# Two key groups in the two row halves of the array: score matmuls in pairs, three stack buffers, one reduction over two banks

## The chip, the core and the metric

One core of a Trainium2 chip runs the whole program. The metric is the device time of one execution in microseconds, the median of a few runs. TensorE (PE) multiplies matrices and writes to PSUM, which has eight banks of 512 float32 numbers on each of 128 partitions; VectorE (DVE), ScalarE (ACT) and GpSimd (POOL) compute element by element; SyncE (SP) here issues most DMAs. The engines run their own instruction streams in order and meet at semaphores.

## What is computed

Eight images of 256x256 with 32 text tokens each go through a wavelet gate, a first attention with an expert layer, a second attention with an expert layer. Each step adds to the residual `h`, 2304 tokens of 256 numbers. The change touches the second attention only, a grouped one: 16 query heads of 16 dimensions share 4 key/value groups.

```python
def _L1_attn_ref(x, Wq, bq, Wk, bk, Wv, bv, Wo, bo):
    ...
    q = (x @ Wq.T + bq).reshape(b, n, G, hpg, HD)
    k = (x @ Wk.T + bk).reshape(b, n, G, HD)
    v = (x @ Wv.T + bv).reshape(b, n, G, HD)
    scale = 1.0 / jnp.sqrt(jnp.float32(HD))
    scores = jnp.einsum('bqghd,bkgd->bghqk', q, k) * scale
    attn = jax.nn.softmax(scores, axis=-1)
    y = jnp.einsum('bghqk,bkgd->bqghd', attn, v).reshape(b, n, d)
    return y @ Wo.T + bo
```

Here b is 8 (images), n is 288 tokens, G is 4 groups, hpg is 4 heads a group, HD is 16.

## The kernel before

The second attention handles one image at a time, in a pipeline of turns (`turn(it)`), each of NU = 18 units U. In turn `it`, the projections of image `it` are made, the row maxima of image `it - 1`, the exponentials and value products of image `it - 2`, and the divisions of image `it - 3`. The same function `turn` stands in the stream of every engine, and the tables at the file's end (`PR_U`, `VT_U`, `MT_U`, `s_at`, `av_at`, ...) say in which unit each step stands. Turns 0 to 3 and 8 to 10 are written out, turns 4 to 7 are two passes of a loop of two turns.

The steps of an image:

- **Projection** (`project`, six matmuls each for m = 0, 1, 2, L1218 to L1220 by the helper `split3`) into bank 7, read by VectorE into `qf` (L1149); ScalarE rounds it to `qh` (L668) and GpSimd makes the rest `ql` (L462).
- **Stack.** SP writes `qh` and `ql` to DRAM (`scrH`, `scrL`, L337, L338) and reads them back as stacks `QS` (queries) and `KS` (keys), two buffers (L347, L350). A stack has three blocks of 16 rows (high x high, high x low, low x high), so one matmul over 48 rows is a product of near float32 precision; at `MROW` two more rows carry the row maxima and, in `KS`, minus ones. Before the change the matmuls use rows 0 to 95 or all 128, the unused rows being zeros that GpSimd wrote.
- **Row scores** (L1463): stationary 128 columns of `QS`, moving 288 keys, once for each of NS = 36 blocks of 128 query rows, alternately into banks 4 and 5. VectorE reduces each to a column of `MX` (L1139). Two transposes in units 5 and 14 (`MT_U`, L1510) bring the maxima to rows, VectorE splits them into `Mh` and `Ml` (L1154, L1156), and SP takes them through DRAM (`scrM`, L357) into the two rows at `MROW` of `QS` (L359).
- **Scores** (L1481): two a unit, stationary 96 keys, moving 384 queries, into banks 0 and 1 or 2 and 3 by turns. ScalarE reads both in one exponential (L661) into the ring `PR` of 12 slots.
- **Values** (L1524): for each of 12 steps m (group g, key tile kt) four matmuls of 32 columns, side by side in the column tiles, accumulate over kt in bank 6. After the third, ScalarE copies the group to `yr` (L715). The next group waits for that copy. A column of ones in `VA` gives the sums of the exponentials.
- **Division.** ScalarE's queue writes the sums to DRAM and reads them back (L692, L697), VectorE inverts (L1162), ScalarE's queue writes the inverses (L700) and reads them back spread over rows as `recb` in eight loads (L708), GpSimd multiplies and adds (L488, L491) into `yT`. The last image is divided on the way through a spreading matmul (L1505) and VectorE (L1169, L1172, L1177) instead. After six warming matmuls (L1226) the output projection (L1553) starts; it needs the `yT` of all images.

In the first turns (`early`) row scores use banks 4, 5, 0 and 1, and projections banks 2, 3 and 7. A unit's order on TensorE is: the score pair, one row score, values, projection, transposes, the other row score.

## Time and profile before

| | us |
|---|---|
| median of 3 runs | 867.09 |
| lowest and highest | 866.78 to 868.91 |
| the profiled execution | 867.73 |
| its span, first to last instruction | 866.0 |
| TensorE busy | 745.6 |
| VectorE busy | 599.9 |
| ScalarE busy | 347.5 |
| GpSimd busy | 146.6 |

The profile is one execution. A page gives busy times, digits of forty slices of the span and the costliest groups of instructions; the trace gives every instruction in order of time with what ended the idle time before it. Records of matmuls overlap, since they are pipelined, so the distance of two starts says more than a duration. PE is a matmul, PEld the load of its stationary operand. The second attention lies between 364 and 613 us.

### The profile page before, as it was taken

The page shows a single profiled execution, that of the slowest core. Times are in us where ns is not written, and L with a number is a line of the kernel's source. Part 1 is how long each engine was busy: PE and PEld are TensorE (multiplying, and loading weights), DVE is VectorE, ACT ScalarE, POOL GpSimd, SP SyncE. Part 2 cuts the span into 40 slices and gives each one's busy share as a digit, 9 for nine tenths or more (in the row PEclk, how much of TensorE's full clock was granted, in tenths as well). Part 3 has the DMA queues.
Part 4 walks back from the last instruction along what each step waited for, and adds up shares of the span by engine and source line. Part 5 has one row for each costly group of instructions (what it writes and reads, how often), then busy time and mean ns, then how long its engine had stood idle before and what let it go on. Part 6 is the DMA issues. An engine that isn't in the chain of part 4 may idle for free.

```text
span 866.0 us, 14451 instructions
## 1 busy us (share of the span) xinstructions
PE 745.6 (86%) x4818; PEld 631.8 (73%) x4818; DVE 599.9 (69%) x1377; ACT 347.5 (40%) x613; POOL 146.6 (17%) x136
## 2 busy tenths in 40 slices
PE   4549996899999996447999999998766899999997
PEld 4538994699999996335556655553544899999997
DVE  6396667677777778737777767763685777777776
ACT  1305543433333333102766666777155233333332
POOL 0105552000000001346013331112353000000000
PEclk9999996999999998556999999999878999999999
DMA  6300000000000000044345345321300000000000
GB/s 242 123 41 1 1 0 0 1 2 1 1 1 1 0 0 0 1 93 96 83 95 105 87 68 111 86 44 34 167 1 1 1 19 1 19 19 1 20 19 19
DMA packets 21559, 34.77 MB, mean 40 GB/s; under 512 B 6572, under 2 KB 17500, under 8 KB 20960
## 3 DMA queue, kind: packets, MB, share of 16 engines
q1 hardware_dynamic: 16632, 31.60, 13.9%
q10 hardware_dynamic: 4872, 2.46, 1.7%
q8 instruction: 32, 0.52, 0.3%
q14 instruction: 23, 0.19, 0.1%
HBM read 24.03 MB, written 9.99 MB: 39 GB/s over the span
## 4 chain that ended last, share of the span: by engine, by line
PE 72%; DVE 14%; DMA 4%; issue 3%; ACT 3%; POOL 2%; SPq 1%; ACTq 0%; POOLq 0%; DVEq 0%
PE PS L1218 16%; PE PS L1220 15%; PE PS L1219 15%; PE PS L1524 6%; PE PS L1463 5%; PE PS L1481 4%; DVE MX L1139 2%; PE PS L1247 2%; DMA KS<-scrH 1%; DMA scrL<-ql 1%; DVE nmr L1205 1%; PE PS L1306 1%; PE PS L1340 1%; PE PS L1226 1%; DVE stats L851 1%
## 5 line engine op out<-in xcount | busy, mean ns | idle before, releaser
L1139 DVE TENSOR_REDUCE MX<-PS 128x1 f32<-128x288 f32 x288 | 125.1, 452 | 51.7 <-PE PS L1463 48.5
L1071 DVE SCALAR_TENSOR_TENSOR h<-PS,cmb,h 128x256 f32<-128x256 f32 (+1 forms) x342 | 143.8, 476 | 0.3 <-PE PS L1220 0.3
L661 ACT ACTIVATE PR<-PS 96x768 f32<-96x768 f32 x144 | 115.4, 806 | 47.7 <-PE PS L1481 45.3
L629 ACT ACTIVATE sg<-PS 128x384 f32<-128x384 f32 x114 | 55.9, 491 | 166.4 <-PE PS L1220 166.4
L1463 PE MATMUL PS<-KS,QS 96*128 96x288 f32 x288 | 97.8, 360 | 17.9 <-DMA KS<-scrH 15.7
L1056 DVE TENSOR_TENSOR al<-aa,ah 128x384 fp32r<-128x384 f32 x114 | 63.7, 558 | 67.1 <-ACT ah L633 67.1
L1463 PEld LDWEIGHTS PS<-KS,QS 96*128 96x128 f32 x288 | 57.3, 203 | 60.1 <-DVE MX L1139 40.4
L633 ACT ACTIVATE ah<-aa 128x384 fp32r<-128x384 f32 x114 | 60.0, 526 | 83.6 <-DVE aa L1050 83.6
L1050 DVE TENSOR_TENSOR aa<-sg,PS 128x384 f32<-128x384 f32 x114 | 63.2, 555 | 26.5 <-ACT sg L629 25.9
L1220 PE MATMUL PS<-xTl,W1h 128*128 128x384 f32 x240 | 81.0, 337 | 0.0
L1218 PE MATMUL PS<-xTh,W1h 128*128 128x384 f32 x240 | 80.8, 337 | 0.0
L1219 PE MATMUL PS<-xTh,W1l 128*128 128x384 f32 x240 | 80.7, 336 | 0.0
L1481 PE MATMUL PS<-QS,KS 128*96 128x384 f32 x288 | 75.6, 347 | 1.9 <-DVE MX L1139 1.1
L1220 PE MATMUL PS<-xTl,W0h 128*128 (+1 forms) x216 | 73.6, 341 | 0.0
L1219 PE MATMUL PS<-xTh,W0l 128*128 (+1 forms) x216 | 73.3, 340 | 0.0
L1218 PE MATMUL PS<-xTh,W0h 128*128 (+1 forms) x216 | 73.3, 340 | 0.0
L1524 PE MATMUL PS<-PR,VA 128*32 128x288 f32 x768 | 66.3, 418 | 1.1 <-ACT yr L715 1.0
L1218 PE MATMUL PS<-W1h,ah 128*128 128x256 f32 x180 | 51.2, 284 | 4.0 <-DVE al L1056 4.0
L1220 PE MATMUL PS<-W1l,ah 128*128 128x256 f32 x180 | 51.0, 284 | 0.0
L1219 PE MATMUL PS<-W1h,al 128*128 128x256 f32 x180 | 50.6, 281 | 0.0
L1218 PE MATMUL PS<-W0h,ah 128*128 128x256 f32 x162 | 46.1, 285 | 4.4 <-DVE al L1056 4.4
L1481 PEld LDWEIGHTS PS<-QS,KS 128*96 128x96 f32 x288 | 42.2, 165 | 9.8 <-ACT PR L661 4.6
(233 smaller groups left out, 1567.4 us busy)
## 6 DMA issues: line engine op xcount, KB each, us to landing
QS<-scrH SPq DMA_DIRECT2D x32, 144.0 KB, 3.9
W1raw<-in_w SPq DMA_DIRECT2D x1, 3840.0 KB, 11.6
W0raw<-in_w SPq DMA_DIRECT2D x1, 3456.0 KB, 10.7
scrH<-qh SPq DMA_DIRECT2D x8, 432.0 KB, 2.5
scrL<-ql SPq DMA_DIRECT2D x8, 432.0 KB, 3.2
QS<-scrL SPq DMA_DIRECT2D x16, 144.0 KB, 4.5
out_tokens<-h SPq DMA_DIRECT2D x6, 384.0 KB, 2.4
x_in<-in_x SPq DMA_DIRECT2D x2, 1024.0 KB, 6.4
```

The costliest lines, as they stand in the source:

```text
L633: A_(ah[:, b], aa[:, b], ACT.Copy).then_inc(s[f"f{L}_ah"], 1)
L661: A_(PR[0:KT, c0:c0 + 2, :], PS[0:KT, b:b + 2, 0:CW], ACT.Exp).then_inc(s["e_exp"], 1)
L1050: V.tensor_tensor(aa[:, b], sg[:, b], PS[:, 2 + b, 0:GW], ALU.mult).then_inc(s[f"f{L}_mul"], 1)
L1056: V.tensor_tensor(al[:, b], aa[:, b], ah[:, b].bitcast(F32), ALU.subtract).then_inc(s[f"f{L}_al"], 1)
L1071: ins = V.scalar_tensor_tensor(out=hj, in0=PS[:, b + t // 2, (t % 2) * D:(t % 2) * D + D], scalar=cmb[:, ds(g * GT + t, 1), e:e + 1].squee ...
L1139: V.tensor_reduce(MX[:, c // NSH, c % NSH:c % NSH + 1], PS[:, max_bank(it, c), 0:POS], AX_X, ALU.max).then_inc(s["e_mx"], 1)
L1218: M(out_, wh, xh, start=(start and c == 0), stop=False)
L1219: M(out_, wl, xh, start=False, stop=False)
L1220: ins = M(out_, wh, xl, start=False, stop=(stop and c == n - 1))
L1463: M(PS[:, max_bank(it, c), 0:POS], QS[q][0:MROW, c * P:c * P + P], KS[q][0:MROW, c // 9 * POS:c // 9 * POS + POS], start=True, stop=True). ...
L1481: ins = M(PS[0:KT, n % 4, 0:CW], KS[p][:, g * POS + kt * KT:g * POS + kt * KT + KT], QS[p][:, g * HQ + cc * CW:g * HQ + cc * CW + CW], sta ...
L1524: ins = M(PS[32 * hh:32 * hh + 32, 6, 0:POS], VA[p][:, kt, g, :], PR[:, c0:c0 + 3, :].rearrange("p c w -> p (c w)")[:, hh * POS:hh * POS + ...
```

## The change

- **Row halves.** Stacks hold groups 0 and 1 in rows 0 to 49 and groups 2 and 3 in rows 64 to 113 (`TILE` = 64, `MROW` = 48), with half the columns. A score pair is now the same key tile and query columns of groups g and g + 2, each in its half of the array; a row-score pair is block c of both halves. The zeroing of the stacks on GpSimd is gone.
- **Maxima over two banks.** Row scores go in pairs to banks 4 and 5, one pair a unit, and one reduction over both banks writes two columns of `MX`, 9 apart. The next pair waits for it (`e_mx`). In the first turns pairs alternate between banks 4, 5 and 0, 1.
- **Three stack buffers** (`NQB`) and three `yr`. SP writes the minus ones of all three before the first stack, in both halves, reads both halves of a stack at a turn's end after all scores of the image that had the buffer, and reads the maxima back in two pieces.
- **Two rings** in `PR`, of 3 and 5 slots of three chunks; value products follow the order of groups `Y_G` = 0, 2, 1, 3 at the units `AV_U`.
- **Schedule.** Projections are made a turn earlier, in units 10, 12 and 14, so the stage has a turn -1; transposes of the maxima in units 6 and 16; the inverses are read back and the division done a turn later. All turns are written out.

```diff
-RING = 12
+NRA, NRB = 3, 5
+NQB = 3
 NS = NGQ * HQ // P
-MROW = 96
+TILE, MROW = 64, 48
...
-    QS = [seq(f"QS{p}", [P, NGQ * HQ], F32R, cur=k1) for p in range(2)]
-    KS = [seq(f"KS{p}", [P, NGQ * POS], F32R, cur=k1) for p in range(2)]
-    PR = seq("PR", [P, RING, CW], cur=k1)
+    QS = [seq(f"QS{p}", [P, NGQ // 2 * HQ], F32R, cur=k1) for p in range(NQB)]
+    KS = [seq(f"KS{p}", [P, NGQ // 2 * POS], F32R, cur=k1) for p in range(NQB)]
+    PR = seq("PR", [P, (NRA + NRB) * 3, CW], cur=k1)
...
+        for it in range(-1, IMGS + 1):
+            if live(it, 1):
+                max_rows(it - 1, 0)
+            if live(it, -1):
+                stack_out(it + 1)
+            if live(it, 1):
+                max_rows(it - 1, 1)
+            if live(it, -1):
+                if it < 0:
+                    sp.wait_ge(s["e_const"], 2)
+                    for p in range(NQB):
+                        minus_ones(p)
+                stack_in(it + 1, 0)
+                stack_in(it + 1, 1)
...
-                    old = (2 * U + 1 - RING) // 3
-                    wait(act, s["e_avt"], i * NAV + old + 1)
-                    c0 = (2 * U) % RING
+                    G = (i * NU + U) // 3
+                    if U % 3 == 0:
+                        ring_free(G, NRA, 0)
+                        ring_free(G, NRB, 1)
+                    ca, cb = ring_at(G, 0) + U % 3, ring_at(G, 1) + U % 3
                     b = 2 * (U % 2)
-                    A_(PR[0:KT, c0:c0 + 2, :], PS[0:KT, b:b + 2, 0:CW], ACT.Exp).then_inc(s["e_exp"], 1)
+                    A_(PR[0:KT, ca:cb + 1:cb - ca, :], PS[0:KT, b:b + 2, 0:CW], ACT.Exp).then_inc(s["e_exp"], 1)
...
+                if live(it, 4) and not last_image(it - 4) and U in RB_U and it < IMGS + 2:
+                    inverses_in(it - 4, RB_U.index(U))
+            if it == IMGS + 1:
+                for n in range(len(RB_U)):
+                    inverses_in(IMGS - 2, n)
...
+                k, c = s_at(U)
+                if live(it, k):
+                    i, hf = it - k, c // (NSH // 2)
+                    dve.wait_ge(s["e_s"], NSH * i + c + 1)
...
+                    b, z = max_bank(it, c), c % (NSH // 2)
+                    V.tensor_reduce(MX[:, hf, z:z + NSH // 2 + 1:NSH // 2], PS[:, b:b + 2, 0:POS], AX_X, ALU.max).then_inc(s["e_mx"], 1)
...
+        def scores(i, U):
+
+            g, kt, cc = U // 9, U % 9 // 3, U % 3
+            for a in range(2):
+                r = slice(TILE * a, TILE * a + MROW + 2)
+                ins = M(PS[0:KT, 2 * (U % 2) + a, 0:CW], KS[i % NQB][r, g * POS + kt * KT:g * POS + kt * KT + KT],
+                        QS[i % NQB][r, g * HQ + cc * CW:g * HQ + cc * CW + CW], start=True, stop=True, tile_position=(TILE * a, 0))
+            ins.then_inc(s["e_st"], 1)
+
+        def row_scores(i, c, bank):
+
+            g = c // (NSH // 2)
+            for a in range(2):
+                r = slice(TILE * a, TILE * a + MROW)
+                ins = M(PS[:, bank + a, 0:POS], QS[i % NQB][r, c * P:c * P + P], KS[i % NQB][r, g * POS:g * POS + POS],
+                        start=True, stop=True, tile_position=(TILE * a, 0))
+            ins.then_inc(s["e_s"], 1)
...
+                    wait(pe, s["e_mx"], NSH * i + c - (1 if early(it) else 0))
+                    row_scores(i, c, max_bank(it, c))
...
-PR_U = [0, 1, 2]
-VT_U = 3
-MT_U = [5, 14]
-
-SUM_U, SM_U, REC_U, RO_U, RB_U = [1, 2], 4, 7, 8, list(range(10, 18))
-S_LEAD = 8
+PR_U = [10, 12, 14]
+VT_U = 8
+MT_U = [6, 16]
+
+SUM_U, SM_U, REC_U, RO_U, RB_U = [6, 7], 11, 14, 16, list(range(4, 12))
+S_LEAD = 4
+
+Y_G = [0, 2, 1, 3]
+AV_U = [6, 7, 10, 11, 12, 13, 15, 17, 19, 20, 21, 22]
...
 def max_bank(it, c):
-    return (4, 5, 0, 1)[c % 4] if early(it) else 4 + c % 2
+    return (4, 0)[c % 2] if early(it) else 4
```

Three places of the order of instructions follow. In a row "L1441" is a line, then the operation, what it writes and reads, the size and how many stand in a row; a number behind QS or KS names the buffer. In the program after, L1432 are scores, L1441 row scores, L1456 values and L1195 to L1197 projections.

TensorE, before, a turn's first projections, with a score pair between two single row scores:

```order
L1481 MATMUL PS<-QS_140,KS_142 96x384 x2
L1463 MATMUL PS<-KS_141,QS_139 128x288
L1524 MATMUL PS<-PR,VA_144 32x288 x4
L1218 MATMUL PS<-xTh,a1h 128x288
L1219 MATMUL PS<-xTh,a1l 128x288
L1220 MATMUL PS<-xTl,a1h 128x288
...
L1463 MATMUL PS<-KS_141,QS_139 128x288
L1481 MATMUL PS<-QS_140,KS_142 96x384 x2
```

TensorE, after, units 10 and 11 of a turn and the start of unit 12:

```order
L1432 MATMUL PS<-QS_140,KS_143 96x384 x2
L1441 MATMUL PS<-KS_144,QS_141 128x288 x2
L1456 MATMUL PS<-PR,VA_147 32x288 x4
L1195 MATMUL PS<-xTh,a1h 128x288
L1196 MATMUL PS<-xTh,a1l 128x288
L1197 MATMUL PS<-xTl,a1h 128x288
...
L1432 MATMUL PS<-QS_140,KS_143 96x384 x2
L1441 MATMUL PS<-KS_144,QS_141 128x288 x2
L1456 MATMUL PS<-PR,VA_147 32x288 x4
L1432 MATMUL PS<-QS_140,KS_143 96x384 x2
```

The two single row scores of a unit have become a pair, and a value step, the first of a group, now stands one unit behind the projection.

SP, before, the start of the stage:

```order
L337 DMA scrH<-qh 128x864
L338 DMA scrL<-ql 128x864
L347 DMA QS_139<-scrH 16x8x288 x2
L347 DMA QS_139<-scrL 16x8x288
...
L350 DMA KS_141<-scrH 16x2x288
L332 DMA KS_141<-neg_158 2x1152
L332 DMA KS_142<-neg_158 2x1152
L337 DMA scrH<-qh 128x864
```

SP, after, the same place:

```order
L340 DMA scrH<-qh 128x864
L341 DMA scrL<-ql 128x864
L335 DMA KS_142<-neg_161 2x576 x2
L335 DMA KS_143<-neg_161 2x576 x2
L335 DMA KS_144<-neg_161 2x576 x2
L350 DMA QS_139<-scrH 16x8x288 x2
L350 DMA QS_139<-scrL 16x8x288
L354 DMA KS_142<-scrH 16x2x288
L354 DMA KS_142<-scrL 16x2x288
L354 DMA KS_142<-scrH 16x2x288
```

The minus ones, six loads instead of two, have moved from behind the first stack to ahead of it.

ACT, before, the end of the stage, the last inverses among the last exponentials:

```order
L715 ACTIVATE yr_155<-PS 128x288
L708 DMA recb<-scrR 16x2x288
L661 ACTIVATE PR<-PS 96x768
L708 DMA recb<-scrR 16x2x288
L661 ACTIVATE PR<-PS 96x768
L708 DMA recb<-scrR 16x2x288
L715 ACTIVATE yr_155<-PS 128x288
L739 ACTIVATE xnp<-h,nmr,rstd 128x256 x3
```

ACT, after, the same place (L646 is the exponential, L685 the write of the inverses, L699 their load, L705 the copy to `yr`):

```order
L646 ACTIVATE PR<-PS 96x2x384 x3
L685 DMA scrR<-rec 128x36
L646 ACTIVATE PR<-PS 96x2x384
L699 DMA recb<-scrR 16x2x288 x8
L705 ACTIVATE yr_157<-PS 128x288 x2
L724 ACTIVATE xnp<-h,nmr,rstd 128x256 x3
```

All eight loads of the inverses now stand between the last exponential and the last two copies.

## Rows read from the trace of the kernel before

**Rows 1.** The page: granted TensorE clock in forty slices, tenths of full.

```profile
PEclk9999996999999998556999999999878999999999
```

**Rows 2.** Grouped view: what, count, busy us, mean ns, idle before, releasers.

```profile
L661 ACT ACTIVATE PR<-PS 96x768 f32<-96x768 f32 x144 | 115.4, 806 | 47.7 <-PE PS L1481 45.3
...
L1524 PE MATMUL PS<-PR,VA 128*32 128x288 f32 x768 | 66.3, 418 | 1.1 <-ACT yr L715 1.0
```

**Rows 3.** Timeline of TensorE, one unit: start, length, engine, line, what, count.

```profile
446.10 0.69 PE L1524 MATMUL PS<-PR,VA 128*32 128x288 f32 x8
446.72 0.40 PE L1463 MATMUL PS<-KS,QS 96*128 96x288 f32 x1
446.96 0.51 PE L1481 MATMUL PS<-QS,KS 128*96 128x384 f32 x2
447.31 0.29 PE L1463 MATMUL PS<-KS,QS 96*128 96x288 f32 x1
447.54 0.69 PE L1524 MATMUL PS<-PR,VA 128*32 128x288 f32 x8
```

**Rows 4.** Timeline at the same place: reductions and next load, idle before.

```profile
447.16 0.94 DVE L1139 TENSOR_REDUCE MX<-PS 128x1 f32<-128x288 f32 x2 [0.49 <-PE PS L1463]
...
448.15 0.19 PEld L1463 LDWEIGHTS PS<-KS,QS 96*128 96x128 f32 x1 [0.47 <-DVE MX L1139]
```

**Rows 5.** Timelines of TensorE, VectorE and ACT: a projection and its followers.

```profile
434.61 0.40 PE L1218 MATMUL PS<-xTh,a1h 128*128 128x288 f32 x1
...
435.53 0.30 PE L1463 MATMUL PS<-KS,QS 96*128 96x288 f32 x1
...
435.73 0.52 DVE L1149 TENSOR_SCALAR qf<-PS,bq 128x288 f32<-128x288 f32 x1 [1.00 <-PE PS L1220]
...
436.29 0.44 ACT L668 ACTIVATE qh<-qf 128x288 fp32r<-128x288 f32 x1 [1.11 <-DVE qf L1149]
436.64 0.39 ACT L715 ACTIVATE yr<-PS 128x288 f32<-128x288 f32 x1
```

**Rows 6.** Chain that ended last, the stage's start: start, length, what.

```profile
371.15 3.17 DMA scrL<-ql
376.60 4.65 DMA KS<-scrH
381.30 3.22 PE PS L1463 x9
...
400.88 0.62 PE PS L1463
...
405.32 0.93 PE PS L1481 x2
```

**Rows 7.** Timeline of SP's queue at the stage's start.

```profile
377.07 0.90 SPq L347 DMA_DIRECT2D QS<-scrH  x2
...
379.89 1.36 SPq L332 DMA_DIRECT2D KS<-neg  x2
...
391.36 0.37 SPq L337 DMA_DIRECT2D scrH<-qh  x1
```

**Rows 8.** Timeline, the last turn's start and the stage's end.

```profile
583.71 0.95 PE L1481 MATMUL PS<-QS,KS 128*96 128x384 f32 x4
...
602.30 0.59 PE L1481 MATMUL PS<-QS,KS 128*96 128x384 f32 x2
602.73 0.65 PE L1505 MATMUL PS<-yr,spread 128*128 128x288 f32 x2
...
603.42 1.96 DVE L1169 RECIPROCAL qf<-PS 128x288 f32<-128x288 f32 x1 [2.16 <-PE PS L1505]
...
608.07 1.30 PE L1505 MATMUL PS<-yr,spread 128*128 128x288 f32 x2 [3.58 <-DVE qf L1172]
...
613.00 7.17 PE L1553 MATMUL PS<-wo,yT 128*128 128x256 f32 x30
```

**Rows 9.** DMA view: issues, KB each, median us from issue to landing.

```profile
scrR<-rec ACTq DMA_DIRECT2D x7, 18.0 KB, 1.9
```

More of the change, by code:

```diff
@@ L237, in build @@
     xn1 = at("xn1", [P, 2, GT, D], F32, k1[0])
-    yr = [seq(f"yr{p}", [P, NGQ, POS], cur=k1) for p in range(2)]
+    yr = [seq(f"yr{p}", [P, NGQ, POS], cur=k1) for p in range(3)]
     SW = NGQ * HPG * POS // P
@@ L725, in _ @@
+        for it in range(-1, IMGS + 3):
+            turn(it)
         n1 = sum(WCOLS[1]) // NG
@@ L1466, in turn @@
+        def turn(it):
+            for U in range(NU):
                 if live(it, 2):
@@ L1531, in _ @@
         pe.wait_ge(s["e_hi"], NG)
-        for it in range(4):
-            turn(it, it % 2)
-        with pe.Fori(2, 4) as r:
-            last[0] = ("e_msplit", 2 * (2 * r - 1))
-            turn(2 * r, 0)
-            turn(2 * r + 1, 1)
-        last[0] = ("e_msplit", 14)
-        for it in range(8, 11):
-            turn(it, it % 2)
+        for it in range(-1, IMGS + 3):
+            turn(it)
         warm_up(3)
```

344 lines of the change are left out of this document (146 added, 198 removed).

## Prediction

> **What bounds the kernel now.** I read the page first, then the timeline of the second attention, engine by engine. That stage runs from 364 to 613 us; nothing outside it is edited. Its clock is full except at its start: the digits of PEclk fall in slices 16 to 19 (of 21.65 us) and stay at 9 from slice 20 to 28 [rows 1]. It is a pipeline of turns, one image each, of 18 units. A unit issues two score matmuls (L1481, read by ACT's exponential), two row-score matmuls (L1463, read by the row maxima of VectorE, L1139) and, in 12 units of 18, four column-tiled value matmuls (L1524). The seven turns from the first score pair, at 405.32, to that of the last turn, at 584.07 (the second pair of the row at 583.71), take 178.8 us, 25.5 on average [rows 6, 8]. In a unit with values TensorE's starts are 0.62 (values), 0.24, 0.35 (score pair) and 0.23: 1.44 us with no gap [rows 3]. The reader should see beside it that the maxima are just as long: 0.44 us from the load of a row-score matmul to its reduction, two reductions of 0.47, and 0.05 from the end of a reduction to the load that it frees: 1.43 [rows 3, 4]. So two engines bound the turn almost equally, and an edit to one is worth only what the other leaves.
>
> **The steady unit.** The change issues both kinds of pair in the two row halves of the array and reduces both banks of a row pair with one instruction. But banks 4 and 5 are now one buffer: the next row pair waits until the reduction of this one has ended, where before two single banks took turns. The loop is: load and matmul pair 0.44, reduction of 576 numbers, 0.05. For the reduction: 288 numbers take 0.47 [rows 4]. On ACT the exponential of 768 takes 0.806 and a copy of 288 0.39, so 0.87 ns a number; by that slope 288 more make 0.72, and with nothing shared it would be 0.94 [rows 2, 5]. I take 0.76, nearer to the end that has the measured slope. **Cycle: 0.44 + 0.76 + 0.05 = 1.25 us.** No row shows a pair in row halves. The nearest is the value group: eight records of 0.418 us on average lie within 0.69 [rows 2, 3], so column tiles do run side by side; I take the second matmul of a pair at nothing, and keep as bounds 0 and the 0.24 between two successive starts [rows 3]. TensorE then needs 0.62 + 0.25 (score pair: half of 0.35, and 0.08 for the first after values, as 602.30 to 602.73 is 0.43 for a pair [rows 8]) + 0.22 = 1.09: hidden under 1.25. TensorE wins 0.35 a unit with values and the loop takes 0.16 of that back; in units without values two row scores ran at the pace of the reductions, 2 x 0.47, and the loop costs 0.3 more.
>
> The Trainium skill ("TensorE: Matmul & The Clock Gate", Part 3) has row tiles start some 4 ns apart; by it the bound of 0 holds, and no row here shows it.
>
> **A turn with projections, by units.** Units 0 to 9: ten of 1.25 and 0.1 for the split of the maxima in unit 6, 12.6. Units 10 and 12 have values and a projection, and there TensorE is late: 0.22 + 0.62 + 0.92 (434.61 to 435.53 [rows 5]) + 0.09 + 0.25 = 2.10 each. The 0.09 is a change between whole array and halves, priced by 0.23 between a row-score matmul and values against 0.14 between matmuls of as many columns in a row (0.92 for six and the first's 0.24) [rows 3, 5]. Unit 11 starts a new value group, which waits for ACT's yr of the group of unit 10; yr stands behind qh on ACT, and qh behind projection 0. From TensorE free: 0.20 to qf, 0.56 to qh, 0.35 to yr, 0.39 and 0.05 [rows 5], so 1.55; then values 0.62 and score pair 0.25; the row pair of unit 12 comes 2.08 after that of unit 11. Units 13 to 17: 1.29, 1.48 (projection without values), 1.27, 1.25, 1.33. **Sum 25.5 us.** A turn without projections: 18 x 1.25 + 0.2 = 22.7.
>
> The Trainium skill ("TensorEngine Tiling (Array Packing)", Key Properties) says a change of tiling mode drains TensorE, which speaks against this change: some nine more a turn. By the rows, where 0.23 against 0.14 agrees with it, six lie in units where TensorE is hidden; without the other three, at 0.09 in five turns, the sum would be 1.4 us lower.
>
> **The seven turns up to the last.** Before: 178.8 us, six of them with projections. After: projections move a turn ahead, so five have them: 26.5 (1.0 more while the clock is still at its lower level), 4 x 25.5, 22.7, and 21.1 for the turn whose last four units have no row scores: 172.3. **-6.5.** Last turn, no maxima in either: 18.2 before (584.07 to 602.30); the narrower score pairs take 0.17 from 17 units, and ACT's exponentials floor it near 14: 15.5. **-2.7.**
>
> **The start.** SP now writes six rows of minus ones, 0.68 each from 1.36 for two, 4.1, where it waited 2.8 for scrL (371.15 + 3.17, less the 0.43 of its issue): +1.3. The first row pair needs both halves of image 0, 12 loads, not 6, 0.47 each: +2.8 [rows 6, 7]. So it starts at 385.4, not 381.3. Of image 1 only projection 2 is then left: its stack goes out at 389.6, not 391.4, and with six loads more lands at 401.9 (400.9 before); four row pairs with a projection between take 5.3, to 407.2 against 405.3 [rows 6, 7]. **+1.9.** POOL's clearing of PR doubles (32x9216), and its low halves of image 2 come behind that and behind the eighteen additions of bo; the second maxima of image 0 and the stack of image 2 hang on them, and I put both just before units 9 and 14 of the first turn want them. I take 0 and keep 3.
>
> In steady turns SP starts 12 loads at a turn's end; at 0.47 each and 4.65 to land [rows 6, 7] they take 10 of the 17 us to unit 14, so three buffers only keep this hidden. The maxima of a half land some 6 us after unit 16, and unit 9 of the next turn is 14 us away.
>
> **The end.** Inverses of image 6 are loaded a turn later. In the last turn all eight loads stand on ACT behind the last exponential and ahead of two yr copies. The write of the inverses is issued at unit 16 and lands 1.9 later [rows 9]; eight issues of 0.42, as SP's, keep ACT until 5.3 us after the last score pair; then yr 0.45, two value groups, the spreading matmul with 0.6, a reciprocal of 1.96 and its product 0.5, which brings the second spreading to 10.2; its 4.9 to the output projection (608.07 to 613.00) make 15.1. Before: 613.00 - 602.30 = 10.7 [rows 8]. **+4.4.** POOL's divide (done at 11.5) and the load of W1 slip by as much and stay hidden.
>
> **Sum.** -6.5 - 2.7 + 1.9 + 4.4 = -2.9. The profiled execution took 867.7, the median is 867.1; 867.1 - 2.9 = 864.2, and I forecast **864.0**.
>
> **Rivals.**
> (a) The halves' loads run one after the other: the second stands in each loop, at the 0.10 by which a row-score matmul with its load in the open (0.24) exceeds one in a stream (0.14). About 100 units run at the loop's cycle: +10, 874. For it: loads of these two lines do show one by one now. Against: the value group again.
> (b) **Slower outright**: the pair isn't concurrent at all. Then the loop is 1.25 + 0.24 = 1.49 and TensorE 1.50: 100 x 0.25, and 0.41 in three units of five turns, and the 2.7 of the last turn are lost: +34, 898. This decides from 0.03 us a pair on: 100 x 0.03 eats the gain. Against it: the value group.
> (c) A shorter loop: reduction at 0.70 and 0.05 less in the matmuls' way, 1.14, where TensorE's 1.09 comes next: -11, 853. For it: ACT's slope.
> (d) The clock falls in steady turns, since TensorE idles in most units. The record has PEclk at 9 through the last turn, with waits in it [rows 1], and lower ones where whole us are empty. At 1.2 GHz a unit with values needs 1.9 and not 1.25: over 60 us more, 925.
>
> **Numbers.** Forecast 0.58 (own range 857 to 872: start 0 to 3, end 2 to 6, each loop +-0.05), (a) 0.13, (b) 0.10, (c) 0.14, (d) 0.05. The range 851 to 877 leaves out (b) and (d), 0.15. 0.3% is 2.6 us, about what a measurement of this kernel can tell from no change. Faster by more, under 864.5: all of (c) and half of the forecast, 0.43. Within: 864.5 to 869.7, 0.17. Slower: a quarter of the forecast, (a), (b), (d): 0.40.
>
> **What would show it.** Right: reductions of two banks near 0.76 us, 1.25 from row pair to row pair in ordinary units, TensorE's idle time before row pairs put down to the maxima, about 2.1 for units 10 to 12, turns of 25.5 and 22.7, output projection 15 us after the last score pair. Wrong: matmuls of a pair 0.11 or 0.24 apart (a, b), a granted clock under 1.0 between 430 and 590 us (d), loops under 1.2 (c), or the stack's loads as the releaser of a row pair in steady turns.

## The result, and the profile after

The kernel after takes **882.05 us** (median of four runs, 881.36 to 886.67), the kernel before took 867.87 in the same comparison (866.78 to 868.91). The ratio is 1.0173, with a 95% interval of 1.0152 to 1.0194: slower by 1.7%, where 864.0 with a range of 851 to 877 was forecast. The profiled executions take 882.37 and 867.73, so the traces differ by 14.6.

The page first, its granted TensorE clock, to be held against [rows 1]:

```profile
PEclk9999997999999996555799978999778999999999
```

A slice is now 22.0 us long. Of the slices that stood at 9 up to the end of the turns, the twentieth and the twenty-fourth are at 7 and the twenty-fifth is at 8; low stretches of a few us hardly show at this grain. Next the groups that the forecast was about (what, count, busy us, mean ns, idle before and releaser), against [rows 2]:

```profile
L1122 DVE TENSOR_REDUCE MX<-PS 128x2 f32<-128x576 f32 x144 | 108.1, 756 | 79.8 <-PE PS L1441 79.5
...
L1456 PE MATMUL PS<-PR,VA 128*32 128x288 f32 x768 | 76.9, 477 | 9.5 <-ACT yr L705 8.6
```

The reduction over two banks has the 0.76 us of the forecast. But the value matmuls, which nobody edited, rose from 418 to 477 ns on average. The timeline of TensorE (start, length, line, what, count, idle before) shows how, against [rows 3]:

```profile
445.61 0.42 PE L1432 MATMUL PS<-QS,KS 50*96 50x384 f32 x2
446.08 0.40 PE L1441 MATMUL PS<-KS,QS 48*128 48x288 f32 x2
446.31 0.34 PE L1432 MATMUL PS<-QS,KS 50*96 50x384 f32 x2
447.33 0.40 PE L1441 MATMUL PS<-KS,QS 48*128 48x288 f32 x2 [0.68 <-DVE MX L1122]
447.66 1.18 PE L1456 MATMUL PS<-PR,VA 128*32 128x288 f32 x8
...
452.06 0.69 PE L1456 MATMUL PS<-PR,VA 128*32 128x288 f32 x8 [0.73 <-ACT yr L705]
```

Three things stand here. Both matmuls of a pair lie in 0.40 us, what one took before: the row halves do run side by side. Row pair follows row pair after 1.25 us (446.08, 447.33), to the hundredth the forecast cycle, and TensorE waits 0.68 us for the reduction. And right behind that wait the eight value matmuls take 1.18 where they took 0.69: TensorE has dropped to the lower of its clock's two levels (1.2 and 2.4 GHz). At 452.06 it is back. The windows of 20 us (PE, weight loads, VectorE, ACT and POOL busy with counts, then granted clock, DMA share, GB/s) show the same from above:

```profile
460.00:480.00 20.00, 16.65 (x136) 7.15 (x136) 11.71 (x19) 12.15 (x21) 0.80 (x1) 0.91 0.62 120
480.00:500.00 20.00, 18.32 (x159) 8.58 (x157) 13.23 (x22) 13.39 (x21) 5.74 (x5) 1.00 0.51 102
500.00:520.00 20.00, 17.29 (x135) 8.25 (x133) 11.41 (x19) 11.61 (x21) 6.53 (x6) 0.90 0.36 87
520.00:540.00 20.00, 18.20 (x112) 8.32 (x108) 8.67 (x13) 9.34 (x16) 0.79 (x1) 0.59 0.42 58
```

The same timeline gives each turn its length: the transposes of V, once a turn, start at 416.04, 445.15, 473.48, 499.35, 529.90, 558.81 and 581.62. The turn from 473.48 takes 25.9 and the one without projections 22.8, against 25.5 and 22.7 in the forecast; the other four take 28.3 to 30.6.

**Where the 14.6 us are**, by the two traces:

| stretch | before | after | difference | forecast |
|---|---|---|---|---|
| up to the stage's first projection | 364.35 | 356.51 | -7.8 | 0 |
| from there to the first score pair | 41.0 | 45.7 | +4.7 | +1.9 |
| seven turns, up to the last | 178.8 | 190.5 | +11.7 | -6.5 |
| last turn | 18.2 | 17.0 | -1.2 | -2.7 |
| last score pair to the output projection | 10.7 | 16.6 | +5.9 | +4.4 |
| the rest of the program | 253.0 | 254.3 | +1.4 | 0 |

Two rows are wrong by far more than a term's uncertainty, in opposite directions: the turns (forecast 18.2 us too low) and the work ahead of the stage (7.8 too high). The experiments ask for the cause of each.

### The profile page after: what moved, and what is told of

It is laid out like the page before. It is cut to its first block, busy times and chain, and to the rows that moved or that the text cites. A ratio compares the mean times of both kernels' runs of the same rounds, so it can differ in the third digit from the quotient of the medians.

```text
span 880.6 us, 13415 instructions
## 1 busy us (share of the span) xinstructions
PE 747.0 (85%) x4818; PEld 604.5 (69%) x4818; DVE 574.7 (65%) x1233; ACT 344.7 (39%) x613; POOL 139.9 (16%) x132
## 3 DMA queue, kind: packets, MB, share of 16 engines
q1 hardware_dynamic: 16712, 31.61, 14.4%
## 4 chain that ended last, share of the span: by engine, by line
PE 73%; DVE 15%; ACT 4%; issue 3%; SPq 1%; DMA 1%; POOL 1%; ACTq 1%; DVEq 0%; POOLq 0%
PE PS L1195 16%; PE PS L1197 16%; PE PS L1196 16%; PE PS L1456 7%; PE PS L1441 5%; DVE MX L1122 4%; PE PS L1432 4%; PE PS L1224 2%; DVE nmr L1182 1%; PE PS L1317 1%; DVE stats L836 1%; PE PS L1215 1%; PE PS L1203 1%; DMA halves<-in_halves 1%; PE PS L1283 1%
## 5 line engine op out<-in xcount | busy, mean ns | idle before, releaser
L1122 DVE TENSOR_REDUCE MX<-PS 128x2 f32<-128x576 f32 x144 | 108.1, 756 | 79.8 <-PE PS L1441 79.5
L646 ACT ACTIVATE PR<-PS 96x768 f32<-96x768 f32 x144 | 112.1, 803 | 42.7 <-PE PS L1432 40.4
L1441 PE MATMUL PS<-KS,QS 48*128 48x288 f32 x288 | 61.1, 426 | 35.0 <-DVE MX L1122 18.7
L1456 PE MATMUL PS<-PR,VA 128*32 128x288 f32 x768 | 76.9, 477 | 9.5 <-ACT yr L705 8.6
L1195 PE MATMUL PS<-xTh,W1h 128*128 128x384 f32 x240 | 81.2, 338 | 0.0
L1197 PE MATMUL PS<-xTl,W1h 128*128 128x384 f32 x240 | 81.2, 338 | 0.0
L1441 PEld LDWEIGHTS PS<-KS,QS 48*128 48x128 f32 x288 | 33.2, 228 | 59.2 <-DVE MX L1122 36.9
L1197 PE MATMUL PS<-xTl,W0h 128*128 (+1 forms) x216 | 73.3, 339 | 0.0
L1195 PE MATMUL PS<-xTh,W0h 128*128 (+1 forms) x216 | 73.2, 339 | 0.0
L1432 PE MATMUL PS<-QS,KS 50*96 50x384 f32 x288 | 63.6, 441 | 2.9 <-ACT PR L646 1.5
L1432 PEld LDWEIGHTS PS<-QS,KS 50*96 50x96 f32 x288 | 25.5, 174 | 51.3 <-issue 27.2
L1195 PE MATMUL PS<-W1h,ah 128*128 128x256 f32 x180 | 51.6, 287 | 4.0 <-DVE al L1041 4.0
L1197 PE MATMUL PS<-W1l,ah 128*128 128x256 f32 x180 | 51.4, 286 | 0.0
L1195 PE MATMUL PS<-W0h,ah 128*128 128x256 f32 x162 | 46.4, 286 | 4.6 <-DVE al L1041 4.6
```

The source lines that it names most:

```text
L646: A_(PR[0:KT, ca:cb + 1:cb - ca, :], PS[0:KT, b:b + 2, 0:CW], ACT.Exp).then_inc(s["e_exp"], 1)
L1122: V.tensor_reduce(MX[:, hf, z:z + NSH // 2 + 1:NSH // 2], PS[:, b:b + 2, 0:POS], AX_X, ALU.max).then_inc(s["e_mx"], 1)
L1195: M(out_, wh, xh, start=(start and c == 0), stop=False)
L1197: ins = M(out_, wh, xl, start=False, stop=(stop and c == n - 1))
L1432: ins = M(PS[0:KT, 2 * (U % 2) + a, 0:CW], KS[i % NQB][r, g * POS + kt * KT:g * POS + kt * KT + KT], QS[i % NQB][r, g * HQ + cc * CW:g * H ...
L1441: ins = M(PS[:, bank + a, 0:POS], QS[i % NQB][r, c * P:c * P + P], KS[i % NQB][r, g * POS:g * POS + POS], start=True, stop=True, tile_posi ...
```

## Experiments

Each ratio is to the kernel before, measured beside it on the same chip. The texts of what was expected speak of three theories: 1, TensorE's idle time lowers its clock; 2, the waits alone cost the time; 3, matmuls of 48 rows in the halves count for less than whole ones.

### Is it the clock, and does filling TensorE's idle time cure it?

Fillers are matmuls whose results the score pair overwrites. In the kernel after:

```diff
                     wait(pe, s["e_exp"], i * NU + U - 1)
+                    if it <= IMGS and (U in FILL_U or U == 15 and not live(it, -1)):
+                        for f in range(FILL_N):
+                            M(PS[:, 2 * (U % 2) + f % 2, 0:CW], a1h[:, 0, 0:P], xTh[:, 0, 0:CW], start=True, stop=True)
+FILL_U, FILL_N = (1, 6, 9, 10, 17), 3
```

> The kernel after with 15 to 18 matmuls a turn that add nothing (three of 128x384 ahead of the score pairs of units 1, 6, 9, 10 and 17, where the row pair behind them waits for the reduction; also of unit 15 in the two turns without projections; their results are overwritten by the score pair). Theory 1, the clock: TensorE's idle gaps of 0.68 us in the units without values let the chip lower TensorE's clock again and again; the four turns of the after trace that take 28.3 to 30.6 us go back to about 25.9, the granted clock stays at full from 440 to 590 us, and the time falls by some 14 us to about 868. Theory 2, waits in the turn and not the clock: the time stays at 882 or rises by what the fillers delay the pairs. Theory 3, matmuls of 48 rows count for less than those of 96: fillers are a sixth of the work, so the low stretches stay or are half gone, 875 to 882.

Measured: 870.36 us (867.15 to 876.39, ten runs), ratio 1.0029 (1.0006 to 1.0052). Fifteen matmuls a turn **more** make the kernel about 12 us faster. The granted clock is full from 424.7 us to 595.4, in the last turn, and from 473.11 two turns end at 525.28: 26.1 each.

```profile
480.00:500.00 20.00, 19.94 (x169) 10.29 (x165) 13.36 (x22) 13.74 (x22) 5.76 (x5) 1.00 0.51 101
500.00:520.00 20.00, 18.94 (x158) 9.95 (x156) 12.04 (x20) 12.45 (x23) 6.58 (x6) 1.00 0.28 71
520.00:540.00 20.00, 18.94 (x157) 10.30 (x159) 12.38 (x21) 12.69 (x23) 3.65 (x4) 1.00 0.54 84
```

So what the turns lost behind the first is the clock's. Theory 2, waits alone, falls. The first turn of scores still starts at half clock here.

### Three small moves

Minus ones ahead of the first stack's write in SP's queue; the copies to `yr` ahead of `qh` on ScalarE; the last eight inverses in SP's queue.

```diff
+        sp.wait_ge(s["e_const"], 2)
+        for p in range(NQB):
+            minus_ones(p)
         for it in range(-1, IMGS + 1):
...
+                for k, n in y_at(U):
+                    if live(it, k):
+                        y_raw(it - k, n)
                 if U in PR_U and live(it, -1):
...
-            if it == IMGS + 1:
-                for n in range(len(RB_U)):
-                    inverses_in(IMGS - 2, n)
```

> The kernel after with three instructions moved: the minus ones are written by SP before it waits for the first stack and not behind it, ScalarE copies yr ahead of qh in unit 10, and the eight loads of the inverses of image 6 stand in SP's queue, not in ScalarE's ahead of the last two copies. Theory 1 (the clock takes the largest part, these three the rest): start -4, unit 11 -0.7 in five turns, tail -4.4, in sum -9 to -12, 871 to 873, with slow stretches of TensorE as before. Theory 2 (the clock is a symptom of the late start and the stalls): the slow stretches go too and the time comes to 862 or less.

Measured: 872.98 us (866.36 to 877.84, ten runs), ratio 1.0055 (1.0023 to 1.0088), and its page still has the low stretches. Of the three, the start's expected 4 us did not come: SP's queue shows the first load behind the write of `scrL` either way (start, length, what):

```profile
364.48 0.42 SPq L341 DMA_DIRECT2D scrL<-ql  x1
368.63 0.80 SPq L350 DMA_DIRECT2D QS<-scrH  x2
```

and in the kernel after

```profile
363.48 0.43 SPq L341 DMA_DIRECT2D scrL<-ql  x1
363.95 4.02 SPq L335 DMA_DIRECT2D KS<-neg  x6
368.02 0.87 SPq L350 DMA_DIRECT2D QS<-scrH  x2
```

The six writes were hidden behind the landing of `scrL` all but 0.4 us (4.15 and 4.54 us from its write to the first load). The other two moves did their part: a turn at full clock takes 24.95 (transposes of V at 475.63 and 500.58) against 25.87, and the end is shorter by some 3 us (below). The run alone doesn't split its 9 us between moves and luck with the clock; its ten runs spread over 11 us.

### Both together

> Both edits, the fillers and the three moves. Theory 1: the gains add, -14 and -11, to about 857, which would be 10 us under the kernel before. Theory 2 or 3: no better than the three moves alone, about 872.

Measured: 864.57 us (861.48 to 867.94, ten runs), ratio 0.9965 (0.9947 to 0.9983). Expected 857. It beats the kernel before by 0.35%, clock full from 419.8 us to 607.5, with turns of 25.2 us. What is left is the first turn of scores, at half clock from its start at 401.3 up to 419.8.

The end of the stage in this run, where all inverses went to SP's queue:

```profile
594.51 0.60 PE L1434 MATMUL PS<-QS,KS 50*96 50x384 f32 x4
598.95 0.75 PE L1509 MATMUL PS<-yr,spread 128*128 128x288 f32 x2
...
608.11 9.41 PE L1534 MATMUL PS<-wo,yT 128*128 128x256 f32 x36 [3.05 <-DVE yT L1160]
```

From the last pair (0.26 behind the start of that row) to the output projection 13.3 us, where the kernel after has 16.6, with this on ScalarE:

```profile
615.09 0.41 ACT L705 ACTIVATE yr<-PS 128x288 f32<-128x288 f32 x1 [3.72 <-issue]
615.65 2.15 PE L1456 MATMUL PS<-PR,VA 128*32 128x288 f32 x16 [3.53 <-ACT yr L705]
```

The 3.72 us of issuing eight loads ahead of the copy are the forecast's term; what it did not hold is that TensorE then ran sixteen value matmuls at half clock, in 2.15 us where two groups of eight take some 1.3 at full clock (0.62 and 0.69).

### Idle time alone: the kernel before with gaps

The kernel before, whole-array tiles, with one wait made longer:

```diff
-                    wait(pe, s["e_mx"], NS * i + c - (3 if early(it) else 1))
+                    wait(pe, s["e_mx"], NS * i + c - (3 if early(it) else 0 if c % 2 and U % 3 == 2 else 1))
```

> The kernel before with one longer wait: in the six units a turn without values the second row score waits for the reduction just ahead of it, so the pair of maxima is 0.49 us longer there and TensorE, with matmuls of 96 and 128 rows only, idles about 0.6 us in the same number of units as in the kernel after. By itself 6 x 0.49 x 7.5 turns, +22 us, 889. Theory 1 (idle gaps lower the clock whatever the rows): the granted clock falls in steady turns as in the kernel after and 10 to 20 us more are lost, 899 to 909. Theory 3 (it is the 48 rows): the clock stays full from 430 us and the time is 889.

Measured: 881.29 us (881.18 to 883.36), +13 and not +22, and the granted clock is 1.00 in every window from 420 to 620 us. Gaps of 0.55 us at most, in about as many units as in the kernel after (0.68 there, and 0.7 to 1.0 once a turn), do **not** lower the clock here.

Both row scores of those six units (`0 if U % 3 == 2 else 1`):

> The kernel before with both row scores of six units a turn waiting for the reduction ahead of them, where the last run had one: two passes of 0.96 us against TensorE's 0.82 of work, so it idles 1.1 us in six units of eighteen, more than in the kernel after. With one such wait the time was 881.3; the second adds about as much again, 894. Theory 1: with gaps this long the granted clock falls in steady turns even with full rows, and the time is 905 or more. Theory 3: the clock stays full from 430 us, and 894 stands.

Measured: 902.4 us (two runs), ratio 1.039. Still full clock:

```profile
500.00:520.00 20.00, 17.37 (x127) 10.30 (x129) 12.36 (x29) 11.16 (x21) 6.50 (x6) 1.00 0.43 91
520.00:540.00 20.00, 17.63 (x130) 10.38 (x130) 11.62 (x27) 10.96 (x20) 6.54 (x6) 1.00 0.31 55
```

TensorE's busy share, 17.37 of 20, is that of a window of the kernel after in which the clock falls (17.29 at 0.90). So this busy share, in which the latencies of matmuls count as busy, doesn't tell by itself; at this point theory 1 looked wrong and theory 3, the halves, right.

### The halves alone

The kernel with gaps (881.3), row scores over 48 rows in place of 96. The maxima then lack the third block.

```diff
-                    M(PS[:, max_bank(it, c), 0:POS], QS[q][0:MROW, c * P:c * P + P], KS[q][0:MROW, c // 9 * POS:c // 9 * POS + POS],
+                    M(PS[:, max_bank(it, c), 0:POS], QS[q][0:48, c * P:c * P + P], KS[q][0:48, c // 9 * POS:c // 9 * POS + POS],
```

> The kernel before with one longer wait in six units, which took 881.3 at full clock, and with row scores over 48 rows, not 96 (the third block, low times high, is left out of the maxima); all columns, instructions and waits are the same. Theory 1: rows don't matter, 881 and full clock from 430 us. Theory 3: the clock falls now and then in steady turns as in the kernel after, 886 or more.

Measured: **1082.34 us** (1082.0 to 1083.83). Not 5 us but 200. The clock stays at half for the whole stage, though TensorE hardly waits:

```profile
520.00:540.00 20.00, 19.45 (x67) 10.26 (x65) 6.07 (x14) 6.10 (x12) 6.51 (x6) 0.50 0.30 71
```

Is it the number of rows or the half tile? By the way these programs are built, a matmul of up to 64 rows goes to a tile of 64x128 and a longer one to the whole array; no trace names the tile, what the runs show is the step between two numbers of rows. Two more runs from the unchanged kernel before, over rows 0 to 63 and 0 to 71 (again with part of the third block left out):

> The kernel before, all its waits unchanged, but the row scores over rows 0 to 63 of the stack, not 0 to 95 (part of the third block is left out of the maxima). A matmul of 64 rows or fewer is built for the row half of the array, one of more for the whole array. If the run with 48 rows (1082 us, half clock from 384 to 811) fell because a single half-array matmul between whole-array ones keeps the clock down (theory 3), this one falls as well: over 1000. If it needed the added waits too: 867 to 900.

> The same with rows 0 to 71, eight rows more, which keeps the whole array. Theory 3 in the form that the half tile and the change of tiling matter: 867 as the kernel before, full clock from 420. In the form that the number of rows matters: the clock falls here as well, 880 to 1080.

Measured: with 64 rows 1059.1 and 931.8 us in two runs, with 72 rows 868.64 us (eight runs), ratio 1.0012 (0.999 to 1.0033). Eight rows decide over 60 to 190 us. The pages:

```profile
PEclk9999989999999555555555555555588889999999
```

for 64 rows and

```profile
PEclk9999996999999999556999999999978999999999
```

for 72. A lone matmul of 64 rows among longer ones keeps the clock down, and the clock comes back (at 774.7 us) only behind the last row score (770.96). What it is in them isn't shown. One rival is time in which nothing streams: in the 64-row run a row score is followed by a score pair after 0.53 us (500.61 to 501.14), where its 288 columns need 0.24 at this clock. No run takes that apart from the half tile itself.

### Do halves in pairs count as fillers?

The fillers of the first experiment as pairs of 48 rows in both halves, at the same places and for the same time:

> As the kernel with fillers, in the same places and as long, but each filler is a pair of 48 rows in the two halves of the array, like the score pairs, not one matmul of 128 rows. Theory 1 (only idle time of TensorE counts): same as with full fillers, clock full from 440 us on, 868 to 872. Theory 3 (matmuls of 48 rows count for less than full ones): low stretches come back, 874 to 882.

Measured: 872.72 us (869.93 to 873.14), ratio 1.005 (1.003 to 1.007), clock 1.00 in the turns from 421.8 us. Pairs in both halves fill the time as well as whole-array matmuls: 872.7 and 870.4 differ by less than the first kernel's own spread. So the half tile as such isn't the cause in the kernel after; only a half that stands **alone** kept the clock at half, and the kernel after has none.

### Then why did the gaps do nothing in the kernel before?

What is left is that a pair does the work of two matmuls in the time of one, so TensorE streams columns for less of the time than in either run with gaps. Per unit with values, by rows: two row scores and two scores in 0.24 + 0.35 + 0.23 before, one pair of each in 0.25 + 0.23 after (452.68, 452.93, 453.16). Take the kernel before down the same way: every row score of the steady turns waits for the reduction ahead of it (`0` in place of `1`), and then each reduction is made twice.

```diff
+                    if not early(it):
+                        V.tensor_reduce(MX[:, c // NSH, 64 + c % NSH:65 + c % NSH], PS[:, max_bank(it, c), 0:POS], AX_X, ALU.max)
                     V.tensor_reduce(MX[:, c // NSH, c % NSH:c % NSH + 1], PS[:, max_bank(it, c), 0:POS], AX_X, ALU.max).then_inc(s["e_mx"], 1)
```

> The kernel before with every row score of the steady turns waiting for the reduction just ahead of it: 1.92 us a unit, turns of some 34.6, about 935 in all at full clock. TensorE works about as small a share of the time as in the kernel after (two row scores 0.24, two scores 0.32, values 0.5 of 1.92), all in whole-array or column tiles. Theory A (TensorE does too little in a given time, whatever the tiles): the clock falls in steady turns as in the kernel after, 950 or more. Theory B (the halves are needed for it): full clock from 430 us, 935.

Measured: 962.19 us (two runs), ratio 1.1099, and whole-array tiles now show what the kernel after showed:

```profile
PEclk9999988999999965689989996898897899999999
```

```profile
505.05 0.40 PE L1463 MATMUL PS<-KS,QS 96*128 96x288 f32 x1 [0.19 <-DVE MX L1139]
506.00 0.40 PE L1463 MATMUL PS<-KS,QS 96*128 96x288 f32 x1 [0.55 <-DVE MX L1139]
506.23 0.51 PE L1481 MATMUL PS<-QS,KS 128*96 128x384 f32 x2
506.94 0.40 PE L1463 MATMUL PS<-KS,QS 96*128 96x288 f32 x1 [0.20 <-DVE MX L1139]
```

Its waits are no longer than those of the 902 us run with its full clock, 0.20 and up to 0.55 us ahead of row scores in both; there are only more of them: between 440 and 560 us 65 waits ahead of row scores, 35 of them of 0.20, where the other has 43 and 14.

> The same with each reduction of the steady turns made twice (the first time into unused columns): 0.44 + 0.94 + 0.05 for each row score, 2.86 us a unit, turns of 51.5, about 1055 at full clock, and TensorE idle more than half of the time in whole-array tiles. Theory A: the clock is at half for most of the stage. Theory B: full clock, 1055. If the last run stays full and this one falls, A holds with an edge between them.

Measured: 1082.28 us (two runs), and the clock is at half for most of the stage:

```profile
520.00:560.00 40.00, 31.85 (x136) 16.42 (x137) 22.00 (x56) 12.45 (x21) 6.56 (x6) 0.63 0.26 53
```

**Theory A holds: the halves aren't needed.** In whole-array and column tiles too, the less of the time TensorE streams in these runs, the more of the stage its clock is low. The kernel after looks the same, its clock falls now and then, and matmuls added to its idle time hold it. That what took it there is the pairs, which do their work in half the time, is argued from this and not isolated: its changes between tilings take streaming time as well (last section). The Trainium skill has this case: "TensorE: Matmul & The Clock Gate", in the section on a second failure mode (psum-queue depth-cycling), says that many very short idle times between groups of matmuls make the clock go to and fro. The traces agree, with waits of 0.68 to 1.0 us in the kernel after, and 0.20 to 0.55 in the run of 962 us.

### More idle time in the kernel after

One part of the change undone: two reductions of one bank in place of one over two.

> The kernel after with one part undone: the two banks of a row pair are reduced by two instructions, 0.94 and not 0.76, so the loop is 1.43 and not 1.25 and TensorE idles 0.18 more in nearly every unit: 882 + 100 x 0.18 = 900 if the clock falls no more often than in the kernel after. If idle time between pairs in halves is what lowers it (theory 1, with the halves as its condition), low stretches take most of the stage: 925 or more.

Measured: 885.96 us (883.51 to 888.41), ratio 1.022 (1.0177 to 1.0264). Neither 900 nor 925. The two reductions overlap: they start 0.31 apart and the second takes 0.44, so together 0.75 us where one over both banks takes 0.76. The loop hardly grew; a turn takes 26.7 (534.05 to 560.75) against 25.9. One instruction over two banks is worth 0.8 us a turn at most. As a test of idle time this run is inconclusive, since it hardly added any.

```profile
546.37 0.40 DVE L1122 TENSOR_REDUCE MX<-PS 128x1 f32<-128x288 f32 x1
546.68 0.44 DVE L1123 TENSOR_REDUCE MX<-PS 128x1 f32<-128x288 f32 x1
547.17 0.19 PEld L1442 LDWEIGHTS PS<-KS,QS 48*128 48x128 f32 x2 [0.37 <-DVE MX L1123]
```

### How many fillers, and the first turn

The kernel of 864.6 us with one filler where it has three:

> The kernel of 864.6 us (fillers and three moves) with one filler of 128x384 where it has three. If the clock is near its edge in the kernel after, one filler holds it too, and the turn saves what three cost beyond the idle time: 862. If it takes the idle time to be filled: low stretches come back now and then, 867 to 872.

Measured: 862.22 us (857.1 to 865.77, six runs), ratio 0.9914 (0.9883 to 0.9944). One filler in five units a turn (0.16 us, an estimate: half of the 0.32 that 384 columns take at the lower clock) holds the clock in the profiled execution, from 424.2 to 601.7 us: that little is enough there.

The stage's start, first attempt: a filler ahead of every row pair of the first two turns, 36 while TensorE waits for the stack, and the upper half of the first stack read by ScalarE's queue.

```diff
+                    if it < 2:
+                        for _ in range(36 if it == 0 and c == 0 else 1):
+                            M(PS[:, 6, 0:CW], a1h[:, 0, 0:P], xTh[:, 0, 0:CW], start=True, stop=True)
                     wait(pe, s["e_mx"], NSH * i + c - (1 if early(it) else 0))
```

> The kernel with fillers and three moves (864.6), and two edits at the stage's start: fillers ahead of each row pair of the first two turns, 36 of them while TensorE waits for the first stack, and the upper half of the first stack read by ScalarE's queue beside SP's. If the low clock from 377 to 431 us comes from the idle time at the start, it is full from about 375 or 385 us on, the first turn of scores loses nothing, -8, and the stack comes 2.8 us earlier: 854. If the start is held by SP, the stack and VectorE alone, only the 2.8 of the stack: 862.

Measured: 870.95 us (866.53 to 874.44, ten runs), ratio 1.0035: worse than without. Between single pairs of halves fillers backfire:

```profile
383.56 0.69 PE L1501 MATMUL PS<-xTh,a1h 128*128 128x384 f32 x1
384.18 0.61 PE L1458 MATMUL PS<-KS,QS 48*128 48x288 f32 x2
384.71 0.69 PE L1501 MATMUL PS<-xTh,a1h 128*128 128x384 f32 x1
385.33 0.61 PE L1458 MATMUL PS<-KS,QS 48*128 48x288 f32 x2
```

TensorE never waits here, yet its clock stays at half to 427 us. At this clock matmuls of 288 columns in a row start 0.24 apart (379.07, 379.31, 379.55), so 384 columns need 0.32; but from filler to pair it is 0.62, and from pair to filler 0.54. In this alternation each change between whole array and halves costs 0.3 us in which nothing streams; where the filler stands behind a projection and not behind a pair it is 0.13 (380.27 to 380.72, again 384 columns). The Trainium skill's "TensorEngine Tiling (Array Packing)", Key Properties, has the drain at a change of mode; this trace agrees and gives it these sizes at the lower clock. The other two parts of the attempt tested little. The 36 fillers ran at full clock and were done by 370.4, the clock fell at 373.1, and the first pair came only at 378.12. And the second queue for the stack brought 0.4 of the 2.8 us expected: from the write of `qh` to the first pair 14.0 us (364.10 to 378.12), where the run of 864.6 has 14.4 (363.05 to 377.43).

Second attempt: twelve fillers in one block ahead of the first score pair, where TensorE waits anyway, and three in units 1 to 5 of that turn.

> The kernel of 864.6 us with twelve fillers more ahead of the first score pair, where TensorE waits 1.4 us for the maxima, and three in each of the first turn's units 1 to 5. If the first turn is slow only for its clock, the clock comes to full near 405 and not at 431, and for 2 us of fillers some 6 us of the first turn come back: 859. If the change between halves and whole array keeps it low whatever is added: 867.

Measured: 863.07 us (861.19 to 868.02, ten runs), ratio 0.9945 (0.9925 to 0.9966). The block works at once:

```profile
399.88 3.64 PE L1470 MATMUL PS<-xTh,a1h 128*128 128x384 f32 x12
403.45 0.42 PE L1434 MATMUL PS<-QS,KS 50*96 50x384 f32 x2
403.70 0.30 PE L1443 MATMUL PS<-KS,QS 48*128 48x288 f32 x2
```

The pair behind it takes 0.42, full speed, where without the block it took 0.63 for 18 us more (401.3 to 419.8). The gain over 864.6, 1.5 us, is smaller than the spread of either.

Both together, one filler in the later turns and the block:

> The version that should beat both: the three moves, the fillers at the first turn of scores as in the run of 863.1, and one filler in place of three in the turns after it, as in the run of 862.2. If both gains are of their own places they add: 860. If the spread of the run with one filler is the clock falling now and then, this one spreads as well, 857 to 866.

Measured: **860.14 us** (859.34 to 861.3), ratio 0.9921 (0.9896 to 0.9945). It beats both kernels, by 0.8% and by some 2.5%, and its turns are 24.95 us (439.85, 464.80). Its runs spread over 2 us where those of the kernel with one filler alone spread over 9.

### The 7.8 us ahead of the stage

In the trace of the kernel **before**, VectorE (line, what, length) and GpSimd just ahead of the stage:

```profile
343.95 0.15 DVE L759 TENSOR_TENSOR mt<-stats 128x3 f32<-128x3 f32 x1
344.02 3.93 POOL L448 MEMSET QS<- 128x4608 f32 x1
344.21 4.77 DVE L762 TENSOR_SCALAR mv<-mt 128x3 f32<-128x3 f32 x1
349.11 3.94 POOL L448 MEMSET QS<- 128x4608 f32 x1 [0.15 <-POOL KS L449]
349.24 3.83 DVE L767 TENSOR_SCALAR mt<-mv 128x3 f32<-128x3 f32 x1
```

In the kernel after the first of the long ones takes 0.17 us:

```profile
344.07 0.17 DVE L747 TENSOR_SCALAR mv<-mt 128x3 f32<-128x3 f32 x1
```

An instruction over three numbers a row doesn't take 4.77 us: it stands still while the memset runs. The test puts the zeroing back into the version of 860.1 us, at its old place and as long:

```diff
+        for p in (0, 1, 2, 0):
+            own(nc.gpsimd.memset(QS[p][:, :].bitcast(F32), 0.0))
+            own(nc.gpsimd.memset(KS[p][:, :].bitcast(F32), 0.0))
+            own.settle()
+        pool.sem_inc(s["e_zero"], 1)
```

> The version of 860.1 us with GpSimd's zeroing put back where the kernel before has it: eight memsets of 128 rows, 11520 columns in all, ahead of the first low halves. In the trace of before, VectorE's instructions of 128x3 numbers take 4.77, 4.69 and 3.83 us while these memsets run, and the stage's first projection starts 7.8 us later than in the kernel after. If the memsets hold VectorE up: the same long rows, first projection near 364 and not 356.5, 868 us. If the late start came from something else of the change: no difference, 860.

Measured: 867.08 us (865.11 to 870.1, ten runs), +6.9, with the long rows back:

```profile
344.21 2.01 POOL L445 MEMSET QS<- 128x2304 f32 x1
344.88 1.89 DVE L755 TENSOR_SCALAR mv<-mt 128x3 f32<-128x3 f32 x1
```

So the removed zeroing, costed at nothing, was the change's largest gain: without it the kernel after would stand near 889, an estimate from 882.05 and the 6.9 of this run.

## Why the prediction was wrong

**The steady unit: right.** 0.44 + 0.76 + 0.05 = 1.25 us. The second matmul of a pair costs nothing, the reduction 0.76, the cycle 1.25. Rivals (a), (b) and (c) are refuted by the same rows.

**A turn: right at full clock.** 25.9 and 22.8 against 25.5 and 22.7. The stall in unit 11 is there, 0.72 to 1.0 for `yr`, and moving that copy ahead of `qh` brought 0.9 a turn.

**The seven turns, -6.5: the step that failed.** They came to +11.7. The sum held TensorE's clock at full and gave its fall, rival (d), 0.05. The reason I wrote against it was "lower ones where whole us are empty", read from the digits of the page. The trace of before contradicts it at the stage's start, where thirteen row scores follow each other at the pace of their reductions, 0.37 us apart (busy and counts of PE, weight loads, VectorE, ACT and POOL, then clock, in the two windows):

```profile
393.41 4.98 PE L1463 MATMUL PS<-KS,QS 96*128 96x288 f32 x13 [0.51 <-DVE MX L1139]
392.00:395.60 3.60, 3.05 (x11) 1.75 (x12) 3.51 (x11) 0.00 (x0) 3.60 (x7) 1.00 0.62 246
395.60:398.20 2.60, 2.60 (x8) 2.01 (x7) 2.60 (x8) 0.00 (x0) 2.60 (x5) 0.51 0.89 155
```

The full clock, there since 388.8, fell at 395.6 without a wait longer than 0.82 us in between: no us was empty. Rival (d) named the mechanism rightly, that TensorE idles in most units, but took it as all or nothing: 925 at half clock throughout. It fell for part of the time. 5.7 of the 18.2 us lie in the first turn, 32.2 us (402.20 to 434.35) where the sum had 26.5: the clock came to full at 427.3, in the kernel before at 409.3, and with the block of fillers ahead of it the same turn takes 25.7 (403.45 to 429.18). Of the turns behind it, between the transposes of V at 416.04 and 581.62 stand 165.6 us where the sum has 5 x 25.5 + 22.7 = 150.2 and the last version has 147.6 (414.82 to 562.43). What I failed to ask of a change that halves TensorE's work in a unit is what else reads that work.

**Work ahead of the stage, "the zeroing is gone": costed at nothing, was -7.8.** The rows to see it were in the trace of before; I looked at the stage's own chain and not at who runs beside the instructions removed. Without this miss the total would have been wrong by 26 and not by 18: two errors that partly cancel.

**The start, +1.9, was +4.7.** From the first `qh` to the first row pair 19.6 us against 14.6 (358.88 to 378.45, and 366.72 to 381.30). The twelve loads are there. From the write of `scrL` to the first load 4.54 us stand where 3.18 stood, the +1.3 of the sum, but by luck: only 0.4 of it is the minus ones, and with them moved away the landing is still waited for until 4.15, 1.0 longer than before, which no run explains. The 2 us that I expected back between first row pair and first score pair did not come: 23.8 against 24.0, at half clock.

**The last turn, -2.7, was -1.2, the end, +4.4, was +5.9.** At the end the mechanism was right: moving the loads of the inverses away shortened it by 3.2. What the sum had too small there fits the lower clock (granted at half from 615.0 to 625.2): the second spreading matmul starts 12.1 us behind the last score pair, and not 10.2. In the last turn the clock was full. ScalarE is busy there for 14.5 of 17.0 us, near the floor of 14 that I gave; its 2.5 us of waits (0.84 at the most) are where the sum had 1.5.

**Two slips of the prediction's own.** The last turn of the kernel before starts at 584.15 and not 584.07, which changes no term. And a quarter of the forecast's 0.58 with (a), (b) and (d) is 0.425, where 0.40 was given for slower.

## What to carry to other kernels

When a change takes work off TensorE without taking time off the loop, the freed time may cost the clock: ask what share of each stretch TensorE streams after the change, and if a granted clock below full appears, try matmuls whose results are thrown away in the idle places, in blocks, and not one by one between pairs of another tiling. And look for such a stretch in the profile of before: here there was one. Never leave a lone matmul of 64 rows or fewer in a stream of whole-array ones without looking at the granted clock. And when instructions of one engine are removed, look in the trace for those of another that were unusually long beside them.

## What the runs showed of the hardware that was not expected

- The granted clock fell repeatedly with steady waits of 0.20 to 0.55 us (962 us run), and stayed full with fewer waits of the same lengths (902 us run). Neither the longest wait nor the busy share of the windows predicts it.
- Lone row scores over 64 rows between matmuls over more: 1059 and 932 us, over 72 rows 868.6. With both halves in use no such effect (872.7 with fillers as pairs). What the chip sees of a lone half these runs don't tell.
- A change between halves and whole array costs up to 0.3 us at the lower clock (0.62 and 0.54 against 0.32 and 0.24), and 0.13 behind a projection. At full clock 0.23 stand from a projection to a score pair (475.47 to 475.70, run of 864.6) against 0.14 between projections, the 0.09 of the forecast. But from a row pair to a score pair, both in halves, it is 0.23 too (446.08 to 446.31), and behind a row pair that had waited for its load 0.33 to a projection (477.19 to 477.52) and to values alike (473.72 to 474.05). So at full clock the change can't be told from a pair's own loads.
- Memsets of GpSimd over 128 rows hold up VectorE's small instructions on SBUF (4.77 us where 0.17 is needed). Reductions from PSUM ran on in 0.76 us beside a memset of 32x9216 (382.43 to 390.2, run of 870.95). The Trainium skill's "GPSIMD Engine Reference", Specifications, has the two engines share their interfaces to SBUF, with contention for VectorE's instructions in a two-port mode or with two SBUF inputs; the trace agrees that the two get in each other's way; which of the two conditions the rows above meet it doesn't show.
- Left open: how much of the kernel after's low clock goes back to the drains between tilings and how much to the waits. Both take streaming time away, and no run separates them.
